# A metaformer block whose work order inside one pipeline slot is rearranged

## The reference

```python
def ln_c(v):                       # over channels, eps 1e-6
    return (v - mean(v, 1)) / sqrt(var(v, 1) + eps)
x = x + window_attention(ln_c(x))  # x read as (B, H, W, C) = x.shape without a transpose, 8x8 windows, 4 heads of 16
t = tokens(x)                      # (B, H*W, C)
p = softmax(ln_t(t) @ router_w + router_b); top_p, top_i = top_k(p, 2); top_p /= sum(top_p)
t = t + sum_k top_p[k] * (ln_t(t) @ expert_w[top_i[k]] + expert_b[top_i[k]])   # 8 experts of 64x64
```

## Time and profile before

| | |
|---|---|
| median of three runs | 1271.76 us |
| profiled execution | 1272.42 us |
| its span | 1270.6 us |
| busy PE / PEld / DVE / ACT / POOL | 1190.2 / 732.3 / 1037.2 / 947.5 / 1081.3 us |
| TensorE clock granted, mean of the span | 0.973 |
| DMA | 91.43 MB, 72 GB/s mean |

### The profile page before, as it was taken

The page is one execution under the profiler, slowest core; times in us unless marked ns, Lnnn a source line. Parts: engine busy times, 40 slices in busy tenths (PEclk is TensorE's granted clock), DMA queues, the critical chain, the costliest instruction groups (busy, mean ns, idle before and its releaser), DMA issues.

```text
span 1270.6 us, 47630 instructions
## 1 busy us (share of the span) xinstructions
PE 1190.2 (94%) x19840; PEld 732.3 (58%) x19840; DVE 1037.2 (82%) x2247; ACT 947.5 (75%) x1743; POOL 1081.3 (85%) x925
## 2 busy tenths in 40 slices
PE   4579999999999999999999999999999999999986
PEld 3356566655556665665565666566566655666531
DVE  3448888888888888888888888889888888888864
ACT  8367888878778888877776888887777777777732
POOL 6267999998888999998888899999988888888753
PEclk8589999999999999999999999999999999999988
DMA  6002333322223233232222323322222222222221
GB/s 184 23 21 70 95 85 82 94 70 54 59 65 83 75 88 102 74 76 62 54 63 62 96 78 91 99 71 63 60 71 54 63 61 70 67 58 63 61 70 42
DMA packets 95623, 91.43 MB, mean 72 GB/s; under 512 B 26929, under 2 KB 62385, under 8 KB 95409
## 3 DMA queue, kind: packets, MB, share of 16 engines
q1 hardware_dynamic: 95408, 88.37, 27.5%
HBM read 35.90 MB, written 17.83 MB: 42 GB/s over the span
## 4 chain that ended last, share of the span: by engine, by line
PE 67%; DVE 9%; POOL 8%; DMA 7%; ACT 4%; issue 4%; DVEq 0%; POOLq 0%; SPq 0%; ACTq 0%
PE bank_y L530 16%; PE bank_s L410 9%; PE bank_t L425 7%; PE bank_s L384 6%; PE bank_o L464 4%; DMA r_b<-recip_rows 4%; PE bank_g L518 3%; PE bank_p L518 3%; PE bank_p L454 3%; PE bank_o L438 3%; DVE prob L880 3%; PE bank_t L362 2%; DMA recip_rows<-r_out 2%; PE bank_t L394 2%; POOL prob L1123 2%
## 5 line engine op out<-in xcount | busy, mean ns | idle before, releaser
L1145 POOL TENSOR_TENSOR t_g<-t_t,g_copy 128x512 f32<-128x512 f32 x192 | 245.8, 1293 | 50.2 <-ACT g_copy L713 49.8
L530 PE MATMUL bank_y<-t_g,w_exp 128*64 128x512 f32 x1024 | 270.2, 620 | 10.1 <-POOL t_g L1145 8.9
L1123 POOL TENSOR_TENSOR prob<-prob,mx 128x512 f32<-128x512 f32 x256 | 261.8, 1044 | 19.2 <-DVE mx L887 19.1
L676 ACT ACTIVATE prob<-prob 128x512 f32<-128x512 f32 x256 | 153.1, 625 | 111.4 <-POOL prob L1123 111.3
L680 ACT ACTIVATE prob_t<-bank_t 128x512 f32<-128x512 f32 x256 | 152.4, 596 | 52.7 <-PE bank_t L425 52.7
L992 DVE TENSOR_TENSOR t_g<-t_t,bank_p 128x512 f32<-128x512 f32 x256 | 174.4, 681 | 17.5 <-PE bank_p L518 12.2
L880 DVE TENSOR_TENSOR prob<-bank_s,rel 128x1024 f32<-128x1024 f32 x128 | 156.3, 1221 | 27.6 <-PE bank_s L410 22.6
L425 PE MATMUL bank_t<-idn,prob 128*128 128x128 f32 x1024 | 163.9, 283 | 7.5 <-ACT v_bd L671 4.0
L410 PEld LDWEIGHTS bank_s<-k_m,q_t 32*64 32x64 f32 x4096 | 113.9, 135 | 91.3 <-issue 58.6
L887 DVE TENSOR_REDUCE mx<-prob 128x16 f32<-128x1024 f32 x128 | 155.4, 1214 | 2.3
L425 PEld LDWEIGHTS bank_t<-idn,prob 128*128 128x128 f32 x1024 | 115.8, 142 | 58.7 <-ACT prob L676 30.7
(11 more groups left out here) (122 smaller groups left out, 2325.3 us busy)
## 6 DMA issues: line engine op xcount, KB each, us to landing
t_t<-t_rout SPq DMA_DIRECT2D x256, 128.0 KB, 2.3
x_in<-in_x SPq DMA_DIRECT2D x68, 256.0 KB, 3.3
r_b<-recip_rows SPq DMA_DIRECT2D x64, 256.0 KB
out_y<-y_out SPq DMA_DIRECT2D x128, 128.0 KB, 2.6
r_in<-sum_b SPq DMA_DIRECT2D x64, 16.0 KB
recip_rows<-r_out SPq DMA_DIRECT2D x64, 16.0 KB, 1.7
t_g<-in_sel SPq DMA_DIRECT2D x1, 512.0 KB, 3.7
rel<-in_relb SPq DMA_DIRECT2D x1, 256.0 KB, 3.0
```

The costliest lines, as they stand in the source:

```text
L530: mm(B_Y[C * a:C * a + C, :], w_exp[:, pair, :], t_g[:, (2 * pair + a) % TG, :], start=False, stop=(pair == MIXES // 2 - 1), skip_group_ch ...
L676: A(prob[:, i], prob[:, i], ACT.Exp).then_inc(p_ready.sem, 1)
L1123: G.tensor_tensor(sc, sc, mx[:, i, :].unsqueeze(2).broadcast_to([P, 2 * HEADS, NTOK]), ALU.subtract).then_inc(s_shifted.sem, 1)
L1145: G.tensor_tensor(t_g[:, u % TG, :], t_t[:, p, u % 2, :], g_copy[:, n, :], ALU.mult).then_inc(tg_pool.sem, 1)
```

## The change

On PE, turn 2 moves ahead of experts 0; experts 0, the first scores and experts 1 follow one another in plain slots (in take slots a take and gates 4 come between scores and experts 1); gates 4 comes behind experts 1 (plain) and gates 6 behind gates 5, after turn 3. ACT's order follows. DVE puts `bias` ahead of `normalise` in slots without a take, takes `total_planes` one slot earlier and the five variance operations over from POOL. POOL multiplies gate 2 ahead of `scale_input` in the SCALES slot, and `centre_tokens` moves between shifts 0 and 1. SP issues the store behind the reciprocals. At the start eight matmuls of 128x128 by 512, whose result is not used, are put behind the first takes, and ACT writes the first squares in the planes' own order, so that the sum reads them with a stride.

```diff
@@ sync, slot
                 if outputting:
                     cut_sums(j - 1)
+                if outputting:
+                    spread_reciprocals(j - 1)
                 if j > 3:
                     store(j - 4)
-                if outputting:
-                    spread_reciprocals(j - 1)
@@ tensor, slot
                 if mixing:
                     gates(j - 3, 2)
                     gates(j - 3, 3)
-                    experts(j - 3, 0)
-                if projecting and not work.take:
-                    scores(j + 1, 1 - p, 0)
                 if attending:
                     turn_probs(j, 2, work)
                 if mixing:
-                    gates(j - 3, 4)
-                if projecting and work.take:
+                    experts(j - 3, 0)
+                if projecting:
                     scores(j + 1, 1 - p, 0)
                 if work.take:
                     take(work.batch, *work.take, 1, j)
+                    if mixing:
+                        gates(j - 3, 4)
                 if mixing:
                     experts(j - 3, 1)
-                if mixing:
-                    gates(j - 3, 6)
+                    if not work.take:
+                        gates(j - 3, 4)
                 if attending:
                     turn_probs(j, 3, work)
                 if mixing:
                     gates(j - 3, 5)
+                    gates(j - 3, 6)
@@ tensor, weights(batch)
+                pe.wait_ge(xt_ready.sem, xt_ready.at(0, 1))
+                for n in range(WARM):
+                    mm(B_Y[:, :], idn[:, :], xt[:, 0:4, :].rearrange("p c h -> p (c h)"), start=True, stop=True)
                 pe.wait_ge(loads, ALL_LOADED)
@@ scalar, first squares (FIRST_SQ is now [p, m, c, h] instead of [p, h, 2 * 4])
+                dst = x_sq[:, :, 4 * m:4 * m + 4].rearrange("p h c -> p c h") if first is None else first[:, m]
+                A(dst, xt[:, bass.ds(plane + (2 * r + m) * 4, 4), :], ACT.Square).then_inc(sq_ready.sem, 1)
@@ scalar, slot
+                if attending:
+                    exps(j, 2)
                 if projecting:
                     copy_q(j + 1, 1 - p)
                 if mixing:
                     copy_gates(j - 3, 2)
                 if attending:
-                    exps(j, 2)
+                    copy_probs(j, p, 2)
                     exps(j, 3)
-                    copy_probs(j, p, 2)
-                if mixing:
-                    copy_gates(j - 3, 4)
                 if routing_on:
                     gate_exp(j - 2)
                 if work.take:
                     take(work.batch, *work.take, 1, B_T[:, :])
+                if mixing:
+                    copy_gates(j - 3, 4)
+                if work.take:
                     square_planes(work.batch, *work.take, 0)
-                if mixing:
-                    copy_gates(j - 3, 6)
                 if attending:
                     copy_probs(j, p, 3)
+                if mixing:
+                    copy_gates(j - 3, 6)
@@ vector, slot
                 if work.step == SQUARES:
                     total_squares(work.batch)
+                    total_planes(work.batch)
                 if work.step == PLANES:
-                    total_planes(work.batch)
+                    variances(work.batch)
...
+                if projecting and not work.take:
+                    bias(j + 1, 0)
                 if outputting:
                     normalise(j - 1)
+                if projecting and work.take:
+                    bias(j + 1, 0)
                 if projecting:
-                    bias(j + 1, 0)
                     maxima(j + 1, 0)
@@ gpsimd, slot (variances, five operations of 128x128, moves to vector)
-                if work.step == PLANES:
-                    variances(work.batch)
...
-                if normalising and not work.sums:
+                if normalising and not work.sums and work.step != SCALES:
                     scale_input(j + 2)
                 if mixing:
                     gate(j - 3, 1 - p, 2)
-                if normalising and work.sums:
+                if normalising and (work.sums or work.step == SCALES):
                     scale_input(j + 2)
...
                 if projecting:
                     shift(j + 1, 0)
-                    shift(j + 1, 1)
                 if outputting:
                     centre_tokens(j - 1, 1 - p)
+                if projecting:
+                    shift(j + 1, 1)
@@
+WARM = 8
```

More of the change, by code:

```diff
@@ L153, in build @@
         y_out = sb("y_out", [P, 4, W])
-        FIRST_SQ = (x_sq, prob[:, 0:2].rearrange("p i h n k -> p (i h n k)").rearrange("p (h x) -> p h x", x=2 * 4))
+        FIRST_SQ = [flat.rearrange("p (m c h) -> p m c h", m=2, c=4) for flat in (
+            x_sq[:, :, :].rearrange("p h x -> p (h x)"), prob[:, 0:2].rearrange("p i h n k -> p (i h n k)"))]
         B_S = ctx.enter_context(nc.psum_tensor("bank_s", [P, 2, BANK], F32))
@@ L620, in take, with square_planes @@
                 A(dst, src.rearrange("p (c h) -> p c h", c=4), ACT.Copy).then_inc(xt_ready.sem, 1)
-            def square_planes(batch, t, r, m, dst=x_sq):
+            def square_planes(batch, t, r, m, first=None):
                 n = batch * GROUPS + t * RING
@@ L627, in square_planes @@
                 act.sem_inc(passed, 1)
-                A(dst[:, :, 4 * m:4 * m + 4].rearrange("p h c -> p c h"), xt[:, bass.ds(plane + (2 * r + m) * 4, 4), :],
-                  ACT.Square).then_inc(sq_ready.sem, 1)
+                dst = x_sq[:, :, 4 * m:4 * m + 4].rearrange("p h c -> p c h") if first is None else first[:, m]
+                A(dst, xt[:, bass.ds(plane + (2 * r + m) * 4, 4), :], ACT.Square).then_inc(sq_ready.sem, 1)
             def first_take(batch, t, r):
@@ L760, in slot @@
                     take(work.batch, *work.take, 1, B_T[:, :])
+                if mixing:
+                    copy_gates(j - 3, 4)
+                if work.take:
                     square_planes(work.batch, *work.take, 0)
+                if attending:
+                    copy_probs(j, p, 3)
                 if mixing:
                     copy_gates(j - 3, 6)
-                if attending:
-                    copy_probs(j, p, 3)
                 if work.take:
@@ L813, in prepare_weights, with sum_squares @@
                 dve.wait_ge(set_dve.sem, SET_DVE)
-            def sum_squares(batch, t, r, src=x_sq):
+            def sum_squares(batch, t, r, src=x_sq[:, :, :]):
                 n = batch * GROUPS + t * RING
@@ L819, in sum_squares @@
                 V.tensor_reduce(sums2[:, :, pair].rearrange("p h o -> p (h o)"),
-                                src[:, :, :], AX.X,
+                                src, AX.X,
                                 ALU.add).then_inc(sq_sums.sem, 1)
             def first_sums(batch, t, r):
-                sum_squares(batch, t, r, FIRST_SQ[r])
+                sum_squares(batch, t, r, FIRST_SQ[r].rearrange("p m c h -> p h (m c)"))
             def total_squares(batch):
@@ L841, in turn_root, with variances @@
                              ).then_inc(root_turned.sem, 1)
-            def first_statistics(batch):
-                total_squares(batch)
-                total_planes(batch)
+            def variances(batch):
                 dve.wait_ge(totals.sem, totals.at(batch, 2))
@@ L856, in first_statistics @@
                 V.tensor_scalar(st[:, 4, :], st[:, 4, :], LN_C_EPS, None, ALU.add).then_inc(variance.sem, 1)
+            def first_statistics(batch):
+                total_squares(batch)
+                total_planes(batch)
+                variances(batch)
                 turn_root(batch)
@@ L1044, in _ @@
             pool.wait_ge(set_pool.sem, 1)
[L1046 to L1050, removed]
-                G.tensor_tensor(st[:, 3, :], st[:, 2, :], st[:, 0, :], ALU.mult).then_inc(variance.sem, 1)
-                pool.wait_ge(variance.sem, variance.at(batch, 2))
-                G.tensor_tensor(st[:, 3, :], st[:, 1, :], st[:, 3, :], ALU.subtract).then_inc(variance.sem, 1)
-                pool.wait_ge(variance.sem, variance.at(batch, 3))
-                G.tensor_scalar(st[:, 4, :], st[:, 3, :], 0.0, 1.0 / C, ALU.max, ALU.mult).then_inc(variance.sem, 1)
-                pool.wait_ge(variance.sem, variance.at(batch, 4))
-                G.tensor_scalar(st[:, 4, :], st[:, 4, :], LN_C_EPS, None, ALU.add).then_inc(variance.sem, 1)
             def deviations(batch):
```

## The result

| | before | after |
|---|---|---|
| median | 1271.76 us (1267.67 to 1273.09, 5 runs) | 1260.29 us (1259.03 to 1260.95, 5 runs) |
| profiled execution / span | 1272.42 / 1270.6 | 1260.29 / 1258.5 |
| TensorE clock granted, mean | 0.973 | 0.985 |

A forecast was written before the change was run, and what follows sets the result against it. PE's own order was taken to bound plain and take slots, with late r_b and POOL's work lengthening others. The terms summed to -23.3 us, from 1272.4 to 1249.1, or 1248.4 against the median; range 1239 to 1261.

The forecast's parts named there:

- Part 1: Slots without a take: bias ahead of normalise and the store behind r_b remove stalls from late r_b; -12.0 us.
- Part 6: Plain slots: 0.15 won on PE against 0.2 lost by gates 6 waiting for ACT's copy; taken as 0.
- Part 2: PLANES slots: five variances move from POOL to DVE, 0.28 each, cutting the excess from 1.80 to 0.13; -5.0 us.
- Part 5: Take slots: one fewer turn from gate to expert pair and an earlier turn 2 win 0.15 each; -3.6 us.
- rival A: Gates 6's wait prevails: plain slots grow by 0.2, take slots win nothing; 1259.6 us, chance 0.25.
- Rival C: POOL becomes the bound of plain slots, each of 38 growing by 0.7; 1275 us, chance 0.04.
- Part 3: SQUARES slots: total_planes behind total_squares on DVE exceeds the idle time, costing 0.85 in each of three; +2.6 us.
- Part 7: The start: new squares layout, warm matmuls and earlier pieces in the first slots; -5.7 us.
- (a): First squares at the start: writing in planes' order is faster, less a dearer strided sum; -2.0 us.
- (b): Warm matmuls at the start: first matmuls run fast, then the clock is low again; -1.7 us.
- (c): First slots: bias no longer waits for r_b and the centre step comes a shift earlier; -2.0 us.
- Part 8: Last slots: no other work covers gates 4 behind experts 1, so POOL's products and experts 3 end later; +2.2 us.

The follow-up runs named there:

- store_ahead: Changed kernel with SP's store ahead of the reciprocals again, bias still ahead of normalise: 1259.91 us (0.9903).
- norm_first: Changed kernel with normalise ahead of bias again in all slots, store still behind r_b: 1266.40 us (0.9945).
- centre_last: Changed kernel with centre_tokens back behind shift 1 on POOL: 1256.69 us (0.9902).
- gates4_first: Changed kernel with gates 4 ahead of experts 1 in plain slots too, on PE and ACT: 1257.10 us (0.9903).
- both: Changed kernel with centre_tokens behind shift 1 and gates 4 ahead of experts 1 in plain slots: 1248.90 us (0.9839).
- early6: As both, plus gates 6 ahead of turn 3 in plain slots, its ACT copy ahead of the fourth probabilities: 1247.85 us (0.9818).
- early6_wait: early6 with POOL held in front of shift 2 in PLANES slots until DVE's variances are done: 1243.88 us (0.9790).
- old_order: Changed kernel with PE and ACT order as before the change and centre_tokens behind shift 1: 1256.17 us (0.9877).
- no_warm: Changed kernel without the eight warm matmuls at the start: 1260.17 us (0.9926).
- old_squares: Changed kernel with first squares and their sums in the layout of before: 1263.22 us (0.9946).
- pool_waits: Changed kernel with POOL held in front of shift 2 in PLANES slots until DVE's variances are done: 1259.08 us (one run).
- early6_act: early6 with mean and its square done by ACT at the end of the SQUARES slot, three operations left on DVE: 1247.09 us (0.9809).

## Why the prediction was wrong in size

The direction and the repair of r_b (Part 1, half of the sum) were right; three other parts account for the miss of about 11: Part 6 by 6.0, Part 2 by 3.9, Part 5 by 1.8; the rest nearly cancels. That 1260.29 still lies inside the range is owed to its upper end, which was drawn for rival A.

**Part 1: right**, also in that DVE's repair is enough. But "Each of the two repairs would do most of the work alone" makes them too much alike: DVE's order does all of it (store_ahead), SP's some 7 of 12 (norm_first).

**Part 6, the step that failed most: "I take 0, the nearest rows pulling to both sides".** The wait that it weighed is there, at the 0.20 that was computed for it. What failed is the gain of 0.15 set against it, and the sentence that 0.79 of POOL's idle covers products 0.7 later and an earlier centre_tokens. Together they took 0.95: in the trace after, nothing is left in front of the power, and plain slots take 17.77 instead of 17.57. Two chains, copy to gates 6 and products to power to tokens, now end so close together that undoing one gains 0.00 or 0.05 and undoing both 0.17 (centre_last, gates4_first, both). With POOL's reserve restored the new order does gain in plain slots, but 0.07 (early6, 17.50), half of the 0.15. Rival A had the size right, +0.2 per plain slot and 1259.6 against 1260.29 measured, though by wiping out the take slots' gain entirely and without Part 2's loss. Rival C, POOL as the bound, is the other half of the mechanism, at 0.2 instead of 0.7.

**Part 2: "On DVE I take 0.28 each".** Right for an idle POOL (0.23 to 0.29), wrong in the place where they were put: beside POOL's shifts two take 1.03 and 1.01. The bound of 0.55 was too low, because both ends were durations of operations, and the price was a wait. Of the 1.32 by which a PLANES slot missed its 17.70, this wait is 1.02 (early6 to early6_wait, 18.78 to 17.76) and Part 6's loss 0.24 (19.02 to 18.78). The Trainium skill, SBUF — State Buffer, Who interferes with whom, says that a DVE instruction with two SBUF inputs contends with a GpSimd instruction that reads SBUF, and one in a two-port mode with GpSimd altogether; whichever comes first blocks the other for the whole instruction. The trace agrees: 1.03 beside a shift, 0.29 without. What the Trainium skill says there speaks against this part and should have been a rival: two waits of up to 1.04 in three slots.

**Part 5: "0.09 plus half of 0.11 is 0.15".** The order on PE gave more, 0.23 (old_order to centre_last), but centre_tokens between the shifts took 0.14 back. In sum 0.08 in the mean. What failed is that POOL "leaves room down to about 18.35 per slot": its busy time does (16.78 in the take slot after), the new order of its work does not.

**Part 3 and Part 4: right** within 0.4, Part 3 in part by luck: in store_ahead and no_warm all three SQUARES slots take 18.23 or 18.24, which is 2.0 over 3 x 17.57; the other 1.0 is late data for DVE's inverses (see below).

**Part 7: right in sum, wrong in its pieces.** (a) -2.0: old_squares gives 2.7 from 0 to the end of slot 3, 2.9 in the median. The strided sum of 1.97 against 1.22 is as computed (1.93). By that, the trace agrees with the note on cachelines under Door 1 in the Trainium skill, SBUF — State Buffer. The loss of 0.75 per sum is hidden: the first projection is 2.6 earlier all the same. (b) -1.7: nothing. The projection ran cold; the clock had fallen 2 us before it, and rival B's condition never arose. The trace agrees with the Trainium skill, TensorE: Matmul & The Clock Gate, HAM oscillation: after 7.17 without a matmul the next group started cold, at 1.2 GHz. (c) -2.0: the remaining 3.1, all behind the first projection, are what subtraction leaves, and the causes named do not explain them. Bias behind normalise (norm_first) makes that stretch 0.6 longer, which is within the scatter. centre_tokens behind shift 1 makes it shorter, not longer: by 1.1 in early6, whose clock is low for as long (32.1 us of the stretch at 1.2 GHz, against 32.2), and by 3.5 in centre_last, with 18.0 us. So the granted clock has a share: the kernels with centre_tokens last take 76.4 with 32.1 us of low clock, 75.5 with 23.9 and 74.1 with 18.0. The kernel before has 36.1, which by these would be worth some 0.6 of the 3.1 (estimate).

**Part 8:** +0.9 instead of +2.2; but the tail, 65.7 before, is 66.6 to 68.1 in the traces of the other kernels with the same last slots, so 2.2 is not excluded.

**Still open:** what the rest of the 3.1 at the start is due to. In the three SQUARES slots (18.24, 18.58 and 18.87) DVE's inverses, which wait for a DMA, began 0.34 and 0.64 later in the longer two; whether total_planes has a place that hides it was not tried.

## What to carry over

When two edits lean on the same reserve (here POOL's 0.79 before the power), subtract both from it before calling either free; and undo them together as well as singly, since two equal limits hide each other. A wait counts only where it ends later than what follows can bear, and its total changes when the reader merely asks later: r_b issued late (store_ahead) left 5.4 us of waits and no loss, r_b issued early (norm_first) 19.3 us of waits and slots that were some 5 longer. Before small operations are moved between DVE and POOL, look at what the other engine runs at that moment: holding POOL for 1.34 us made the slot 0.86 shorter.

## What the runs showed of the hardware

Operations of 128x128 on DVE, between SBUF tiles, take 0.23 to 0.29 alone and 0.94 to 1.03 when they meet one of POOL's shifts of 1.04 (after, pool_waits, early6_act), tensor_tensor and tensor_scalar alike. ACT's square of 128x512 takes 1.22 into every eighth word and 0.63 into neighbouring words. DVE's sum of 1024 elements per partition, eight at a time, takes 1.22 side by side and 1.97 at a stride of 128 words (old_squares, after).
